# GpSimd issues an expert's scatters and the gathers for the expert two ahead by turns

## The reference, cut to what matters

```python
h = x.reshape(-1, 128)                                # 2048 tokens
probs = softmax(h @ router_weight.T)                  # 8 experts
topk_probs, selected = top_k(probs, 2)
# at most 640 tokens of an expert are kept; kept_w are the renormalised weights
expert_inputs = zeros((8 * 640 + 1, 128)).at[dispatch].set(h[st])
pre  = einsum('ech,edh->ecd', expert_inputs, ff_pre_act_weight)
gate = einsum('ech,edh->ecd', expert_inputs, gate_weight)
expert_out = einsum('ecd,ehd->ech', pre * silu(gate), ff_post_act_weight)
updates = eo_flat[dispatch] * kept_w[:, None]
out = zeros((2048, 128)).at[st].add(updates)          # rows are added into the output
```

## Time and profile before

| | us |
|---|---|
| median of 3 runs without the profiler | 385.15 (383.79 to 385.44) |
| span of the profiled execution | 410.6 |
| GpSimd, 40 gathers, busy | 38.7 |
| GpSimd, 40 scatters, busy | 62.9 |
| TensorE busy (matmuls) | 305.2 |
| DVE busy | 290.1 |

### The profile page before, as it was taken

The page is one execution under the profiler, slowest core; times in us unless marked ns, Lnnn a source line. Parts: engine busy times, 40 slices in busy tenths (PEclk is TensorE's granted clock), DMA queues, the critical chain, the costliest instruction groups (busy, mean ns, idle before and its releaser), DMA issues.

```text
span 410.6 us, 5169 instructions
## 1 busy us (share of the span) xinstructions
PE 305.2 (74%) x1465; PEld 212.9 (52%) x1465; DVE 290.1 (71%) x615; ACT 144.4 (35%) x285; POOL 211.5 (52%) x145
## 2 busy tenths in 40 slices
PE   5969996776798669766591866969695959597940
PEld 4635342333344335333261555959594949497940
DVE  5954999999999999999978843646363636362500
ACT  2535963223533353344042003333332323233320
POOL 0632455974455435543714062174848484848664
PEclk9965996887888878988786798978797979798995
DMA  6040024254000000000002011144443333323332
GB/s 186 2 102 0 0 52 102 62 140 164 14 13 0 26 26 0 0 26 26 0 27 77 1 41 26 32 92 76 72 85 59 79 62 86 55 48 43 29 26 25
DMA packets 20756, 20.31 MB, mean 49 GB/s; under 512 B 2624, under 2 KB 14848, under 8 KB 20736
## 3 DMA queue, kind: packets, MB, share of 16 engines
q1 hardware_dynamic: 13184, 14.63, 12.4%
q0 software_dynamic: 7040, 5.25, 10.3%
q10 hardware_dynamic: 512, 0.19, 0.3%
HBM read 10.82 MB, written 5.05 MB: 39 GB/s over the span
## 4 chain that ended last, share of the span: by engine, by line
PE 38%; DVE 25%; issue 13%; another core or an unknown queue 9%; POOL 7%; ACT 4%; DMA 1%; DVEq 1%; POOLq 1%; ACTq 0%
PE psum L1481 10%; DVE ring L518 8%; PE psum L1460 5%; PE psum L1315 5%; DVE ring L509 5%; PE psum L1462 5%; PE psum L1461 4%; POOL ring L1130 4%; PE psum L1298 2%; DVE sm L543 2%; POOL out L1197 2%; DVE xn L457 1%; POOL parts L1119 1%; PE psum L1295 1%
## 5 line engine op out<-in xcount | busy, mean ns | idle before, releaser
L1130 POOL TENSOR_TENSOR ring<-ring,cbc 128x1024 f32<-128x1024 f32 x31 | 74.9, 2416 | 85.7 <-DVE ring L518 85.7
L518 DVE TENSOR_TENSOR_SCAN ring<-ring 128x1024 f32<-128x1024 f32 x32 | 102.6, 3210 | 0.0
L1315 PE MATMUL psum<-ring,cst 128*128 128x512 f32 x128 | 76.4, 729 | 15.4 <-POOL ring L1130 15.3
L1298 PE MATMUL psum<-stack,sel_r 128*128 (+1 forms) x120 | 55.8, 572 | 25.4 <-DVE ring L509 24.7
L1197 POOL DMA_INDIRECT out<-ring,sid x40 | 62.9, 1572 | 16.9 <-issue 11.0
L1180 POOL DMA_INDIRECT ring<-rows,gid x40 | 38.7, 968 | 63.4 <-DVE gid L780 39.5
L817 DVE TENSOR_TENSOR ring<-psum,ring 128x320 f32<-128x320 f32 x64 | 31.4, 491 | 56.0 <-ACT ring L1048 30.6
L1460 PE MATMUL psum<-stack 128*128 128x320 f32 x128 | 47.6, 372 | 27.2 <-issue 16.4
L935 ACT ACTIVATE ring<-psum,nega 128x510 f32<-128x510 f32 x64 | 41.7, 681 | 46.1 <-PE psum L1298 44.4
L1048 ACT ACTIVATE ring<-psum 128x320 f32<-128x320 f32 x64 | 27.9, 438 | 78.7 <-PE psum L1462 50.8
L1298 PEld LDWEIGHTS psum<-stack,sel_r 128*128 128x128 f32 x120 | 25.1, 224 | 53.4 <-DVE ring L509 33.6
(11 more groups left out here) (180 smaller groups left out, 342.4 us busy)
## 6 DMA issues: line engine op xcount, KB each, us to landing
stack<-parts SPq DMA_DIRECT2D x16, 256.0 KB, 3.8
win_s<-in_wg SPq DMA_DIRECT2D x8, 256.0 KB
win_s<-in_w SPq DMA_DIRECT2D x8, 256.0 KB
w_s<-in_w SPq DMA_DIRECT2D x8, 256.0 KB
xt<-in_x SPq DMA_DIRECT2D x4, 256.0 KB, 4.7
out<-xt SPq DMA_DIRECT2D x4, 256.0 KB, 2.3
rows<-xn SPq DMA_DIRECT2D x4, 256.0 KB, 2.3
ring<-rows,gid POOLq DMA_INDIRECT x40
```

The lines of the kernel that those rows point to most:

```text
L518: v.tensor_tensor_scan(hh[:, s].rearrange("p a b -> p (a b)"), da[:, s].rearrange("p a b -> p (a b)"), uu[:, s].rearrange("p a b -> p (a b ...
L1130: g.tensor_tensor(hc[:, s], hh[:, s], cb, ALU.mult).then_inc(s_product, 1)
L1298: ins = mm(bank(to + k), sel, stack[:, half, kind, bass.ts(c, CH)], start=True, stop=True)
L1315: ins = mm(bank(YB), wred[:, o:o + D], hc[:, s, k, :], start=(grp == 0), stop=(grp == NG - 1))
```

## The change

In the body for an expert that also has gathers to issue, the gathers and the scatters now alternate: gather 0, scatter 0, gather 1, scatter 1, and so on to gather 4, scatter 4. The wait for `s_scatter_ids` now stands behind the first gather. The number of DMAs, their sizes, their waits and their buffers are the same; the last two experts, which have no gathers to issue, are as before.

```diff
                 if more:
                     gather_ready(e + 2, b)
-                    for q in range(NQ):
+                for q in range(NQ):
+                    if more:
                         gather(b, q)
-                pool.wait_ge(s_scatter_ids, 2 * e + 2)
-                for q in range(NQ):
+                    if q == 0:
+                        pool.wait_ge(s_scatter_ids, 2 * e + 2)
                     pool.wait_ge(s_weighed, NQ * e + q + 1)
 
                     if q == 0 and above_zero(16 * NQ * e):
```

## The result

The changed kernel takes 426.12 us (median of 4 executions, 424.44 to 431.62) against 384.55 us (383.79 to 385.44) for the kernel before on the same chip: a ratio of 1.1056, with a 95% interval of 1.1016 to 1.1097. Ratios here are formed without the executions of a slower state that the chip has (431.62 us is one), so they are not always the quotients of the medians beside them. The direction and the loop through the fifth gather are as forecast; the size is not. The forecast was +28 us with a range up to 420, and it is +41.6 us. The profiled execution took 424.44 us, of which its span is 422.5; the lines of the scatters and of `turn` have moved to L1198 and L1454, those of `down` to L1482.

What follows compares the result with a forecast made beforehand. GpSimd's back-to-back issuing, 15.8 us a group, was taken as the expert loop's bound. Groups of 20.7 us add 24.5 us over five periods, the tail 3.5: 28 us on 385.15, so 413 us, range 398 to 420.

Steps and rivals of the forecast that it cites:

- the loop through the fifth gather: Group to group: fifth gather's issue, landing, transposition, `gid`, next group; 20.0 us, 20.7 with the clock, against 15.8 before.
- the bound: Expert loop of the kernel before: without the profiler GpSimd issues back to back, 15.8 us a group, and bounds it.
- the sign: Whole kernel: the change makes it slower, given a chance of 0.89.
- Rival A: Expert loop: TensorE's waits are real in every execution, so GpSimd has slack; 385 to 388 us, 9 in 100.
- B: Expert loop: late releases come from gathers in a burst, so spacing them helps; 381 to 382 us, 4 in 100.
- C: Half of the profiled excess is elsewhere, groups of some 18 us before the change; 391 to 399 us, 6 in 100.
- the tightest cover is 0.3 us on the first: First scatter of a group: comes up at 1.3 us, its tile weighed at 0.96, so its wait costs nothing.
- its 3.9 us for the gather: End of the loop: from the five transposed tiles through `gid` to the next group's start, 3.9 us.
- the longer pairs: GpSimd's switching between gathers and scatters: at most 0.6 us a group, costed at nothing.
- the clock: 16 down matmuls after TensorE's wait, on its lower level: 1.3 us a group, half taken, 0.65.
- the landing: From the end of the fifth gather's issue to its tile's transposition: 2.2 us, with ends of 1.6 and 2.7.
- the tail: From the sixth group's start to expert 6's scatters, which wait for the first weighed tile: 3.5 us more.

Runs made afterwards that it cites:

- the second profile: The kernel before, unchanged, profiled once more: 385.22 us, with a span of 383.2 us.
- the execution of 1394.64 us: One of four executions of the changed order with each gather one further ahead (gather 0, gather 1, scatter 0, gather 2 and so on); median 409.92 us.

## Why the forecast had the direction and not the size

**Right: the bound and the sign.** GpSimd bounds the kernel before outside that first profiled execution. The change adds no issuing; it makes the fifth gather late, TensorE waits for it, and with TensorE all that leads to the next `gid`. The last transposition waits for the gather in each group, the pairs are 3.2 to 3.5 us apart against 3.1, and moving one gather alone, or five of them further, moves the time as the loop says. Rival A would have been 385 to 388 us, B 381 to 382, C 391 to 399; each needed groups that have slack in the kernel before, and the second profile of it shows 0.30 to 1.75 us. The Trainium skill, "Perfetto Trace Analysis", section "Summary: the profiler window per engine type", was weighed there for A, since it makes a matmul's reported end an estimate. No run here tests that rule itself; the waits that it was to explain are gone from the second profile.

**Wrong: the step "the tightest cover is 0.3 us on the first".** The first scatter was taken to come up at 1.3 us, to find its tile weighed at 0.96, and to start. In the group at 325.00 the tile is weighed 1.16 us after the group's start (326.16 - 325.00), and the scatter that waits for it starts 0.92 us after that, so 2.1 us after the group's start; over the six groups it is 2.0 to 2.7, on average 2.3. Four gathers stand behind it. The rows had this distance already: `gid` was written at 324.44 and the gather started at 325.40, 0.96 us. The forecast counted it inside its 3.9 us for the gather and then took 0.3 for a waiting scatter. With 13.6 against 14.9 the end of the fifth gather's issue is the largest miss, 5 x 1.3 = 6.6 us. About 1.0 of the 1.3 is the first scatter's wait, 5 us in all; the other 0.3 is the longer pairs, which the forecast had priced (at most 0.6 a group) and left out of its sum. The fifth gather late alone, where this wait is covered, has 13.67, as the forecast's 13.6. With TensorE kept busy the first scatter starts 2.0 to 2.1 us after the group's start, so some 0.2 us of the wait came with the lower clock.

**Mis-sized: the clock.** The forecast took half of 1.3 us, because it could not tell whether the level falls there. It does in each group: from the fifth transposition to the next group it is 5.73 us on average against 4.85 in the sum (0.3 + 3.9 + 0.65), 4.4 us over five groups. Keeping TensorE busy gives back 1.7 us there, more than the whole 1.3. The stretch from the first of the 16 down matmuls on, in the group shown and in the next (length, busy time by engine, granted clock, DMA):

```profile
319.90:323.20 3.30, 3.30 (x28) 3.29 (x28) 1.62 (x3) 0.38 (x1) 0.00 (x0) 0.61 0.21 20
```

```profile
342.58:346.20 3.62, 3.62 (x23) 3.56 (x23) 1.62 (x3) 0.38 (x1) 0.00 (x0) 0.50 0.09 10
```

A granted clock of 0.50 is the lower level (1.2 GHz) throughout; at 0.61 most of the stretch was on it. TensorE had waited 3.10 and 3.31 us for the gather just before.

**Mis-sized: the landing.** From the end of the fifth gather's issue to the transposition it is 2.42 us on average, against 2.2: 1.1 us over five groups. By the fit of the Trainium skill, "DMA: Bandwidth & Descriptors", section "Anatomy of one DMA — SWDGE (gpsimd) path", 2.0 us plus the bytes over 436e3 a us, such a gather would take 2.15 us in all, as an estimate. The trace has 0.99 + 2.42 = 3.4 us from the issue's start to the transposition that waits for it, and the profile's page gives 2.6 us as the median from issue to landing, so the trace does not agree with that reading.

**Mis-sized: the tail.** From the sixth group to the first scatter of expert 6 it was to grow by 3.5 us (its own terms, 21.9 less 18.1, give 3.8); it grows from 18.45 (338.95 to 357.40) to 25.50 (371.17 to 396.67), so by 7.1. Expert 6's fifth tile is transposed at 17.4 instead of 16.1. The 24 down matmuls then take 5.33 us on the lower level, and from the end of the weighing at 395.84 to the scatter at 396.67 it is 0.83 us, not 0.3.

**In the other direction: the kernel before.** Its groups are 16.31 us apart, not 15.8, which takes 2.6 us off the difference. The sum over spans: 5 x (23.07 - 16.31) = 33.8, plus 7.1 in the tail, less 1.6 because the first group starts sooner in this execution (255.81 against 257.40), is 39.3 us, the difference of the two spans (422.5 - 383.2). The medians lie 41.6 us apart; the 2.3 us between is less than the executions of the changed kernel differ among themselves.

**What failed as a method.** The forecast's high end, 420, took the long landing and the low clock, but left the first scatter's wait at nothing because 0.3 us of cover seemed to be left. A margin smaller than the delays that the rows show is no margin: the end of the range should have had a wait there.

## What to carry to other kernels

Where DMAs are issued in order, as on GpSimd here, a DMA's place in the queue sets its start time: ask of the last transfer of a batch when its consumer needs it, and put all that is needed soonest ahead, even where the batch looks unbalanced. When a waiting instruction is put ahead of others, price its wait with the measured distance from the producer's end to the waiter's start, and count it for everything queued behind. When a new wait makes TensorE idle, price the work behind the wait from rows at the lower of the two levels, in full.

## What the runs showed of the hardware

A GpSimd DMA that waits for another engine starts 0.83 to 0.97 us after that engine's instruction ends (in the two groups above 0.89 for `gid`, 0.92 and 0.83 for weighed tiles; 0.96 in the first profile of before); two that wait for nothing are 0.30 us apart. TensorE's granted clock was 0.50 to 0.61 behind waits of 3.1 to 3.3 us, and 1.00 where matmuls of zeros stood ahead of the wait; 16 down matmuls took 3.18 to 3.62 us in the first case and 1.97 in the second. One profiled execution of the kernel before was 27.4 us longer than the other (410.6 against 383.2), with long waits of ScalarE in the expert loop; 3.4 us of it lie ahead of the first gather. Which of an engine, a semaphore or the record was late there stays open, and so does the execution of 1394.64 us.
